# Score stack laid out heads, side, time: six two-sided transfers per batch instead of twelve

## The chip, the cores and the metric

The kernel runs on one core of a Trainium2 chip. The metric is device time in microseconds, the median of several runs. A profile of one more execution comes with it; its span goes from the first to the last instruction.

## The reference

Sixteen batches of a 128 x 256 array `x` pass through masked self-attention with 8 heads, then through a mixture of 8 experts of which the best one per token is taken, and the result is added to `x`. Only the attention's scores touch the change:

```python
q = xt @ Wq.T                                  # queries are keys and values too
scores = scale * einsum('bhqd,bhkd->bhqk', qh, qh)   # dk = 16
logits = (scores * cmask + (1.0 - cmask) * NEG) * rmask
attn = softmax(logits, axis=-1)
ctx  = einsum('bhqk,bhkd->bhqd', attn, qh)
out  = ctx @ Wo.T
...                                            # router, top expert, gate/up/down, x + result
```

## The kernel before

**Stages.** After a short opening comes the attention, a loop of 20 steps (`STEPS`) with eight head positions `h` in each, and after that the expert stage, 23 tiles of 128 tokens. Each engine has its own program written out by hand, and semaphores tie them; nothing is reordered by a scheduler. In step `s` TensorE (PE) computes the scores of batch `s` once to find the row maxima (`scores_for_max`, L572), the scores of batch `s - 2` a second time with mask and maximum folded in (`scores_for_exp`, L584), and the later products of batches `s - 2` to `s - 4`. VectorE (DVE) reduces the maxima (L930), ScalarE (ACT) takes the exponentials (L799) and GpSimd (POOL) splits the queries.

**The stack.** The scores are wanted in float32 precision from bfloat16 matmuls. The masked query `qm` of a batch is split into three bfloat16 parts (`parts`, by POOL at L310 to L316, for batch 0 by DVE at L916 to L922), and a tile `stack` holds in its first 96 partitions six slots of 16 rows. Slot `i` multiplies part `LEFT[i]` on the left side by part `RIGHT[i]` on the right side:

```python
LEFT = (0, 1, 2, 0, 0, 1)
RIGHT = (0, 1, 0, 1, 2, 0)
```

A row of the stack holds side, head, time. Each slot and side is one DMA within SBUF (`stack_part`, L437): SyncE's queue (SP) issues the six of the left side, ACT's queue the six of the right. There are five stacks (`NSTACK`). SP issues them in one row with everything else that it loads or stores: `x`, the mask for all partitions (`cond`), the stack's mask row (L468), the expert weights (L486 on), the hidden rows (L477) and, in steps 3, 7, 11 and 15, a copy of four batches of `x` from HBM to HBM (L481). ACT issues its own between exponentials.

**The maxima.** POOL splits a batch's maxima in two (`split_max`), PE turns them (L563, once in each step, at `h` = 2), DVE copies them to `max_rows` (L937), and ACT writes them with one DMA into rows 97 and 98 of the stack's right side (`write_max`, L827, at `h` = 3). `scores_for_exp` of that batch waits for them at `h` = 0 of the next step. In steps 0 and 1 PE runs fillers (`keep_warm`, L554) between the scores.

Of the kernel before, what the change touches and what calls it, by code (L numbers as in the profile page):

```python
# [7 lines left out]
F32 = mybir.dt.float32  # L8
BF16 = mybir.dt.bfloat16
# [3 lines left out]
ACT = mybir.ActivationFunctionType  # L13
AX = mybir.AxisListType

P = 128
NEG = -1e30
NH = 8
# [9 lines left out]
LEFT = (0, 1, 2, 0, 0, 1)  # L28
RIGHT = (0, 1, 0, 1, 2, 0)
ROWS = 6 * DK  # L30
ROW_MASK = ROWS
ROW_MAX = ROW_MASK + 1
ROWS2 = ROW_MAX + 2

NSTACK = 5
NPARTS = 4
NV = 3
NX = 4
# [4 lines left out]
def adaln_ffn(nc, x, cond, wqT, woT, routerT, guT, dnT, out):  # L43
    B, D, T = x.shape
# [4 lines left out]
    NT = T // P  # L49
# [21 lines left out]
    with ctx:  # L71
        def sb(name, shape, dt=F32):
            return ctx.enter_context(nc.sbuf_tensor(name, shape, dt))
# [7 lines left out]
        bank = [ctx.enter_context(nc.psum_tensor(f"bank{i}", [P, 512], F32)) for i in range(8)]  # L81
# [21 lines left out]
        dn2_sb = sb("dn2_sb", [P, E, T])  # L103

        cond_sb = sb("cond_sb", [B, T])
        mask2 = sb("mask2", [B, 2, NH, T], BF16)
        cond_all = sb("cond_all", [P, NCOND, T])
        x_sb = sb("x_sb", [P, NX, T])
        q_sb = sb("q_sb", [P, NQ, T])
        qm = sb("qm", [P, 2, T])  # L110
        rest = sb("rest", [P, 2, T])
        parts = sb("parts", [P, NPARTS, 3, T], BF16)
        stack = [sb(f"stack{r}", [P, 2, NH, T], BF16) for r in range(NSTACK)]
        v_sb = sb("v_sb", [P, NV, NT, NH, VC])
        row_max = sb("row_max", [P, 2, NH, NT])
        max_parts = sb("max_parts", [P, 2, P], BF16)
        max_rows = sb("max_rows", [2 * NH * NT, 2, P], BF16)
# [18 lines left out]
        start = sb("start", [P, E])  # L136
# [41 lines left out]
        rows_made = sem("rows_made")  # L178
# [10 lines left out]
        mask_made = sem("mask_made")  # L189
# [21 lines left out]
        max_in = sems("max_in", 2)  # L211
# [49 lines left out]
        def there(b):  # L261
            return 0 <= b < B
# [6 lines left out]

            return {0: 2, 1: 1}.get(b, b + 1)  # L270

        stack_rows = [stack[r][:, :, :, :].rearrange("p a h t -> p (a h t)").bitcast(F32) for r in range(NSTACK)]

        def home(n, first, end):

# [8 lines left out]
        def _(pool):  # L284
# [14 lines left out]
            def make_parts(b):  # L299
                k, r = b % 2, b % NPARTS  # L300
                pool.wait_ge(q_copied, q_count(b))
                pool.wait_ge(cond_all_in[b % NCOND], 16 * (b // NCOND + 1))
                if b == 2:
                    pool.wait_ge(first_parts, 2)
                g.tensor_tensor(qm[:, k, :], q_sb[:, b % NQ, :], cond_all[:, b % NCOND, :], ALU.mult).then_inc(qm_made, 1)  # L305
                pool.wait_ge(qm_made, b)
                if b >= NPARTS:
                    old = b - NPARTS
                    pool.wait_ge(stack_in[old % NSTACK], 16 * 12 * (old // NSTACK + 1))
                g.tensor_copy(parts[:, r, 0, :], qm[:, k, :]).then_inc(part0_made, 1)  # L310
                pool.wait_ge(part0_made, b)
                g.tensor_tensor(rest[:, k, :], qm[:, k, :], parts[:, r, 0, :], ALU.subtract).then_inc(rest_made, 1)
                g.tensor_tensor(parts[:, r, 1, :], qm[:, k, :], parts[:, r, 0, :], ALU.subtract).then_inc(parts_made, 1)
                pool.wait_ge(rest_made, b)
                pool.wait_ge(parts_made, 2 * b - 1)
                g.tensor_tensor(parts[:, r, 2, :], rest[:, k, :], parts[:, r, 1, :], ALU.subtract).then_inc(parts_made, 1)  # L316
# [114 lines left out]
                eng.wait_ge(qm_made, b - NCOND)  # L431
            eng.dma_start(cond_all[:, b % NCOND, :], cond[b:b + 1, :].to_broadcast([P, T])).then_inc(cond_all_in[b % NCOND], 16)

        def stack_part(eng, b, side, slot):

            part = (LEFT, RIGHT)[side][slot]
            eng.dma_start(stack[b % NSTACK][slot:ROWS:6, side, :, :],  # L437
                          parts[:, b % NPARTS, part, :]).then_inc(stack_in[b % NSTACK], 16)

        def need_parts(eng, b):  # L440
            if b == 0:
                eng.wait_ge(first_parts, 2)
            else:
                eng.wait_ge(parts_made, 2 * b)
            if b >= NSTACK:
                eng.wait_ge(s2_done, NH * (b - NSTACK + 1))

        def stack_first(eng, side):

            eng.wait_ge(first_hi, 1)  # L450
            for slot in range(6):
                if (LEFT, RIGHT)[side][slot] == 0:
                    stack_part(eng, 0, side, slot)
            for part in (1, 2):
                eng.wait_ge(first_parts, part)
                for slot in range(6):
                    if (LEFT, RIGHT)[side][slot] == part:
                        stack_part(eng, 0, side, slot)

        @block.sync  # L460
        def _(sp):
# [7 lines left out]

            def stack_parts(b):  # L470
                need_parts(sp, b)
                for slot in range(6):
                    stack_part(sp, b, 0, slot)

            def write_row(b):
                sp.wait_ge(gate_made, b + 1)
# [21 lines left out]
            stack_first(sp, 0)  # L498
            load_x(sp, 4)
            load_cond(sp, 4)  # L500
            need_parts(sp, 1)
            for slot in range(6):
                stack_part(sp, 1, 0, slot)
            stack_parts(2)
            for b in range(3):
                read_mask(b)
# [21 lines left out]
        def _(pe):  # L528
# [36 lines left out]
            def scores_for_max(b, h):  # L565
                k, n = b % NSTACK, NH * b + h
                if h == 0:
                    pe.wait_ge(stack_in[k], 16 * 12 * (b // NSTACK + 1))
                if n >= 2:
                    pe.wait_ge(max_done, n - 1)  # L570
                for q in range(NT):
                    mm = t_.matmul(bank[h % 2][:, q * T:(q + 1) * T], stack[k][0:ROWS, 0, h, q * P:(q + 1) * P],  # L572
                                   stack[k][0:ROWS, 1, h, :], start=True, stop=True)
                mm.then_inc(s1_done, 1)

            def scores_for_exp(b, h):
                k, n = b % NSTACK, NH * b + h
                if h == 0:
                    pe.wait_ge(max_in[b % 2], 16 * (b // 2 + 1))
                    pe.wait_ge(mask_in[k], 16 * (b // NSTACK + 1))  # L580
                if n >= 2:
                    pe.wait_ge(exp_done, n - 1)
                for q in range(NT):
                    mm = t_.matmul(bank[2 + h % 2][:, q * T:(q + 1) * T], stack[k][0:ROWS2, 0, h, q * P:(q + 1) * P],  # L584
                                   stack[k][0:ROWS2, 1, h, :], start=True, stop=True)
                mm.then_inc(s2_done, 1)

            def apply_probs(b, g):
# [184 lines left out]
        def _(act):  # L773
# [50 lines left out]
            def write_max(b):  # L824
                k = b % 2
                act.wait_ge(max_copied, b + 1)
                act.dma_start(stack[b % NSTACK][ROW_MAX:ROW_MAX + 2, 1, :, :], max_rows[:, k, :]).then_inc(max_in[k], 16)  # L827

            act.dma_start(wq_sb[:, :], wqT).then_inc(wq_in, 16)
            load_cond(act, 0)  # L830
# [7 lines left out]
            copy_q(2)  # L838
            act.wait_ge(cond_in, 16)
            all_heads = cond_sb[:, :].rearrange("b (o t) -> b o t", o=1).to_broadcast([B, NH, T])  # L840
            a.activation(mask2[:, 0, :, :], all_heads, ACT.Copy, bias=NEG, scale=-NEG).then_inc(mask_made, 1)
            a.copy(mask2[:, 1, :, :], all_heads).then_inc(mask_made, 1)
            need_parts(act, 1)
            for slot in range(6):
                stack_part(act, 1, 1, slot)

            for s in range(STEPS):
                for h in range(NH):
                    if there(s - 2):
                        exponential(s - 2, h)  # L850
                    if h < 2 and s >= 1 and there(s + 1):
                        stack_part(act, s + 1, 1, h + 4)
                    if h == 1 and there(s - 4):
                        copy_hidden(s - 4)
                    if h == 1 and there(s - 3):
                        copy_products(s - 3)
                    if h == 2 and there(s + 3):
                        copy_q(s + 3)
                    if h == 3 and there(s - 1):
                        write_max(s - 1)  # L860
                    if h >= 4 and there(s + 2):
                        if h == 4:
                            need_parts(act, s + 2)
                        stack_part(act, s + 2, 1, h - 4)
                    if h == 5 and there(s - 4):
                        exp_gap(s - 4)
                    if h == 5 and there(s):
                        copy_v(s)
                    if h == 6 and there(s - 3):
                        copy_context(s - 3)  # L870
# [33 lines left out]
        def _(dve):  # L904
# [1 line left out]
            minus_pair = float(np.frombuffer(np.array([0xBF80BF80], np.uint32).tobytes(), np.float32)[0])  # L906

            def minus_rows(k):
                v.memset(stack[k][ROW_MASK:P, 0, :, :].rearrange("p h t -> p (h t)").bitcast(F32), minus_pair).then_inc(rows_made, 1)

            minus_rows(0)
            dve.wait_ge(q_done, 1)
# [20 lines left out]
            def copy_max(b):  # L933
                dve.wait_ge(max_turned, b + 1)
                if b >= 2:
                    dve.wait_ge(max_in[b % 2], 16 * (b // 2))
# [301 lines left out]
```

## Time and profile before

| | us |
|---|---|
| median of 3 runs | 227.4 (227.11 to 230.67) |
| the profiled execution, its own time | 226.16 |
| its span | 224.3 |
| PE busy in the span | 208.8 (93%) |
| DVE, ACT, POOL busy | 145.8, 133.5, 113.9 |

The span is shorter than the execution's own time by 1.9 us that lie before its first and behind its last instruction. Busy times overlap. "SPq" and "ACTq" in the trace are the two engines' queues while they issue a DMA; an engine's queue issues in the program's order, and ACT's own instructions behind an issue start after it.

### The profile page before, as it was taken

Reading aid. Unit: us, or ns where it says so; the run is one execution under the profiler, and the core shown is the slowest. Engines: PE = TensorE matmul, PEld = TensorE weight load, DVE = VectorE, ACT = ScalarE, POOL = GpSimd, SP = SyncE. Lnnn points to the kernel's source line nnn. Section 1 sums busy time; section 2 is a strip of 40 time slices with the busy share of each in tenths; the row PEclk is TensorE's granted clock in tenths of the full one; section 3 lists DMA queues with packets and bytes.
Section 4 is the critical chain, followed back from the end, with each engine's and each line's share of the span. In section 5 each row is a group of like instructions: output and inputs, shape, how many; then the busy total and the mean of one; then the engine's idle time right before and its main releaser. Section 6 shows DMA issues by size and latency. Waiting matters only on the chain.

```text
span 224.3 us, 5401 instructions
## 1 busy us (share of the span) xinstructions
PE 208.8 (93%) x1723; PEld 149.5 (67%) x1723; DVE 145.8 (65%) x403; ACT 133.5 (60%) x298; POOL 113.9 (51%) x212
## 2 busy tenths in 40 slices
PE   6997989999999989999999999988899999999970
PEld 5996757767657747757766775446677777777750
DVE  2886977789789879889788884674763223322330
ACT  2260378888778868888887788772543343334310
POOL 5782775366266346346421001304617777777752
PEclk9999999999999999999999999999999999999995
DMA  6795575879699697786865450002716654543210
GB/s 167 183 187 139 122 211 140 229 214 255 160 226 236 174 254 197 183 222 168 242 195 125 134 157 24 27 27 58 238 43 182 195 147 143 157 138 96 93 43 0
DMA packets 44987, 34.39 MB, mean 153 GB/s; under 512 B 6220, under 2 KB 42975, under 8 KB 44960
## 3 DMA queue, kind: packets, MB, share of 16 engines
q1 hardware_dynamic: 26896, 18.77, 32.1%
q10 hardware_dynamic: 15120, 7.04, 12.9%
q0 software_dynamic: 2944, 8.24, 12.6%
q8 instruction: 15, 0.25, 0.5%
q14 instruction: 12, 0.10, 0.1%
HBM read 16.91 MB, written 7.28 MB: 108 GB/s over the span
## 4 chain that ended last, share of the span: by engine, by line
PE 74%; DMA 8%; DVE 5%; SPq 4%; issue 3%; ACT 2%; POOL 1%; ACTq 1%; POOLq 1%; DVEq 0%
PE bank L572 13%; PE bank L596 12%; PE bank L718 12%; PE bank L584 11%; PE bank L737 4%; PE bank L739 4%; PE bank L617 3%; SPq L437 3%; PE bank L539 2%; PE bank L625 2%; PE bank L606 2%; PE bank L729 2%; DMA stack<-max_rows 2%; DMA stack<-parts 2%; PE bank L709 2%
## 5 line engine op out<-in xcount | busy, mean ns | idle before, releaser
L930 DVE TENSOR_REDUCE row_max<-bank 128x2 f32<-128x512 f32 x128 | 85.2, 684 | 12.0 <-PE bank L572 10.6
L799 ACT ACTIVATE probs<-bank 128x512 f32<-128x512 f32 x128 | 75.5, 598 | 21.4 <-PE bank L584 18.1
L572 PE MATMUL bank<-stack 96*128 96x256 bf16 x256 | 49.4, 274 | 2.6 <-DMA stack<-parts 1.6
L584 PE MATMUL bank<-stack 99*128 99x256 bf16 x256 | 48.3, 272 | 0.9 <-DMA stack<-max_rows 0.8
L572 PEld LDWEIGHTS bank<-stack 96*128 96x128 bf16 x256 | 20.5, 97 | 22.3 <-DVE row_max L930 10.9
L596 PE MATMUL bank<-probs,v_sb 128*32 128x256 f32 x512 | 34.3, 385 | 0.2 <-ACT probs L799 0.2
L305 POOL TENSOR_TENSOR qm<-q_sb,cond_all 128x256 f32<-128x256 f32 x15 | 10.9, 729 | 39.6 <-ACT q_sb L784 38.0
L718 PE MATMUL bank<-gu_sb,gotT 128*128 x92 | 31.0, 460 | 0.0
L584 PEld LDWEIGHTS bank<-stack 99*128 99x128 bf16 x256 | 24.1, 97 | 7.1 <-ACT probs L799 2.9
L554 PE MATMUL bank<-ident 128*128 128x128 f32 x148 | 21.2, 286 | 1.8 <-POOL ident L289 1.6
L596 PEld LDWEIGHTS bank<-probs,v_sb 128*32 128x32 f32 x512 | 13.4, 109 | 12.7 <-ACT probs L799 4.7
L554 PEld LDWEIGHTS bank<-ident 128*128 128x128 f32 x148 | 19.2, 200 | 2.5 <-POOL ident L289 1.6
L718 PEld LDWEIGHTS bank<-gu_sb,gotT 128*128 128x128 f32 x92 | 15.8, 190 | 4.9
L882 ACT ACTIVATE silu<-bank 128x176 f32<-128x176 f32 x23 | 7.3, 317 | 19.5 <-PE bank L718 19.5
L1188 DVE SCALAR_TENSOR_TENSOR act_sb<-silu,stack,bank 128x176 f32<-128x176 f32 x15 | 6.0, 398 | 19.7 <-ACT silu L882 19.7
L401 POOL DMA_INDIRECT out<-stack,put_i x15 | 14.9, 994 | 6.3 <-issue 3.7
L876 ACT COPY gotT<-bank 128x256 f32<-128x256 f32 x23 | 8.6, 373 | 14.9 <-PE bank L709 14.9
L392 POOL DMA_INDIRECT stack<-rows_dram,take_i x15 | 14.5, 967 | 4.6 <-issue 3.7
L392 POOL DMA_INDIRECT got<-rows_dram,take_i x8 | 7.9, 982 | 17.3 <-DVE take_i L1085 9.8
L737 PE MATMUL bank<-dn_sb,actT 128*128 x46 | 13.7, 380 | 0.0
L739 PE MATMUL bank<-dn_sb,actT 128*128 x46 | 13.7, 379 | 0.0
L955 DVE MAX8 top<-h_sb 128x8 f32<-128x8 f32 x16 | 2.7, 170 | 15.2 <-ACT h_sb L818 15.2
(160 smaller groups left out, 316.5 us busy)
## 6 DMA issues: line engine op xcount, KB each, us to landing
stack<-parts SPq DMA_DIRECT2D x96, 64.0 KB, 3.0
stack<-parts ACTq DMA_DIRECT2D x96, 64.0 KB, 3.1
gu_sb<-in_guT SPq DMA_DIRECT2D x8, 352.0 KB, 3.9
rows_dram<-h_sb SPq DMA_DIRECT2D x16, 132.5 KB, 2.3
x_sb<-in_x SPq DMA_DIRECT2D x16, 128.0 KB, 3.7
rows_dram<-in_x SPq DMA_DIRECT2D x4, 512.0 KB, 5.2
cond_all<-in_cond SPq DMA_DIRECT2D x12, 128.0 KB, 4.7
dn_sb<-in_dnT SPq DMA_DIRECT2D x4, 256.0 KB, 3.9
```

What stands on the lines that cost most here:

```text
L305: g.tensor_tensor(qm[:, k, :], q_sb[:, b % NQ, :], cond_all[:, b % NCOND, :], ALU.mult).then_inc(qm_made, 1)
L392: g.indirect_dma_start(home(n, 0, ROW), None, rows, bass.IndirectOffsetOnAxis(ap=take_i[:, n:n + 1], axis=0)).then_inc(got_in[n], 16)
L401: g.indirect_dma_start(out_rows, bass.IndirectOffsetOnAxis(ap=put_i[:, n:n + 1], axis=0), home(n, XROW, ROW), None, bounds_check=TOK - 1, ...
L554: t_.matmul(bank[3][:, 0:P], ident[:, :], ident[:, :], start=True, stop=True)
L572: mm = t_.matmul(bank[h % 2][:, q * T:(q + 1) * T], stack[k][0:ROWS, 0, h, q * P:(q + 1) * P], stack[k][0:ROWS, 1, h, :], start=True, stop ...
L584: mm = t_.matmul(bank[2 + h % 2][:, q * T:(q + 1) * T], stack[k][0:ROWS2, 0, h, q * P:(q + 1) * P], stack[k][0:ROWS2, 1, h, :], start=True ...
L596: mm = t_.matmul(bank[PV][c * VC:(c + 1) * VC, g * T:(g + 1) * T], v_sb[:, b % NV, k, HG * g + c, :], probs[:, HG * g + c, k, :], start=(k ...
L718: mm = t_.matmul(bank[1 + m2][:, 0:I2], gotT[:, m2, k, :], gu_sb[:, k, bass.ds(e, 1), :].rearrange("p a i -> p (a i)"), start=(k == 0), st ...
L737: t_.matmul(bank[4 + m2][:, 0:T], actT[:, m2, 0, :], dn_sb[:, bass.ds(e, 1), :].rearrange("p a t -> p (a t)"), start=True, stop=False)
L739: t_.matmul(bank[4 + m2][:, 0:T], actT[:, m2, 1, :], dn2_sb[:, bass.ds(e, 1), :].rearrange("p a t -> p (a t)"), start=False, stop=True).th ...
L799: a.activation(probs[:, h, :, :].rearrange("p k t -> p (k t)"), bank[2 + h % 2][:, 0:NT * T], ACT.Exp, scale=float(DK) ** -0.5).then_inc(e ...
L930: v.tensor_reduce(row_max[:, b % 2, h, :], bank[h % 2][:, 0:NT * T].rearrange("p (q k) -> p q k", q=NT), AX.X, ALU.max).then_inc(max_done, 1)
```

## The change

A row of a stack now holds head, side, time. One DMA writes both sides of a slot, from the two parts that it names (`stack_slot`): six per batch, of which SP issues slots 0 to 2 and ACT slots 3 to 5. For batch 0 SP takes the even slots and ACT the odd ones. In ACT's loop the three stand at `h` = 5, 6 and 7 of step `s` for batch `s + 2`; before, four stood at `h` = 4 to 7 and two at `h` = 0 and 1 of the next step. The maxima of a batch now lie in two pieces of each head's row, and ACT writes them in two DMAs. Mask rows and fill follow the new order.

```diff
-        def stack_part(eng, b, side, slot):
-            part = (LEFT, RIGHT)[side][slot]
-            eng.dma_start(stack[b % NSTACK][slot:ROWS:6, side, :, :],
-                          parts[:, b % NPARTS, part, :]).then_inc(stack_in[b % NSTACK], 16)
+        def stack_slot(eng, b, slot):
+            left = parts[:, b % NPARTS, LEFT[slot], :]
+            both = bass.AP(left.tensor, left.offset, [left.ap[0], [(RIGHT[slot] - LEFT[slot]) * T, 2], left.ap[1]])
+            eng.dma_start(stack[b % NSTACK][slot:ROWS:6, :, :, :], both).then_inc(stack_in[b % NSTACK], 16)
...
-        def stack_first(eng, side):
-            eng.wait_ge(first_hi, 1)
-            for slot in range(6):
-                if (LEFT, RIGHT)[side][slot] == 0:
-                    stack_part(eng, 0, side, slot)
-            for part in (1, 2):
-                eng.wait_ge(first_parts, part)
-                for slot in range(6):
-                    if (LEFT, RIGHT)[side][slot] == part:
-                        stack_part(eng, 0, side, slot)
+        def stack_first(eng, part):
+            if part == 0:
+                eng.wait_ge(first_hi, 1)
+            for last in (1, 2):
+                for slot in range(part, 6, 2):
+                    if max(LEFT[slot], RIGHT[slot], 1) == last:
+                        eng.wait_ge(first_parts, last)
+                        stack_slot(eng, 0, slot)
...
-                act.dma_start(stack[b % NSTACK][ROW_MAX:ROW_MAX + 2, 1, :, :], max_rows[:, k, :]).then_inc(max_in[k], 16)
+                for q in range(NT):
+                    act.dma_start(stack[b % NSTACK][ROW_MAX:ROW_MAX + 2, :, 1, q * P:(q + 1) * P],
+                                  max_rows[q:2 * NH * NT:NT, k, :]).then_inc(max_in[k], 16)
...
-                    if h < 2 and s >= 1 and there(s + 1):
-                        stack_part(act, s + 1, 1, h + 4)
...
-                    if h >= 4 and there(s + 2):
-                        if h == 4:
+                    if h >= 5 and there(s + 2):
+                        if h == 5:
                             need_parts(act, s + 2)
-                        stack_part(act, s + 2, 1, h - 4)
+                        stack_slot(act, s + 2, SP_SLOTS + h - 5)
```

The two places that the prediction speaks of follow in the order of the instructions. The first is SP's opening, before: the loads of `x`, then the left sides of batch 0 (x6) and of batches 1 and 2 (x12), and those of batch 3 eight rows further down.

```order
L425 DMA x_sb<-in_x 128x256 x4
L437 DMA stack<-parts 16x8x256 x6
L425 DMA x_sb<-in_x 128x256
L432 DMA cond_all<-in_cond 128x256
L437 DMA stack<-parts 16x8x256 x12
L468 DMA stack<-mask 1x16x256 x3
L507 DMA wo_sb<-in_woT 128x128
...
L437 DMA stack<-parts 16x8x256 x6
L468 DMA stack<-mask 1x16x256
```

SP's opening now; the shape 16x16x256 is a slot with both sides.

```order
L426 DMA x_sb<-in_x 128x256 x4
L439 DMA stack<-parts 16x16x256 x3
L426 DMA x_sb<-in_x 128x256
L433 DMA cond_all<-in_cond 128x256
L439 DMA stack<-parts 16x16x256 x6
L467 DMA stack<-mask 1x16x256 x3
L504 DMA wo_sb<-in_woT 128x128
...
L439 DMA stack<-parts 16x16x256 x3
L467 DMA stack<-mask 1x16x256
```

The rows are the same and in the same order, with half as many stack transfers in each group.

The second place is ACT's row in one step of the loop, from the exponential at `h` = 3 to that at `h` = 7, before.

```order
L799 ACTIVATE probs<-bank 128x512
L827 DMA stack<-max_rows 2x16x128
L799 ACTIVATE probs<-bank 128x512
L437 DMA stack<-parts 16x8x256
L799 ACTIVATE probs<-bank 128x512
L437 DMA stack<-parts 16x8x256
L822 ACTIVATE gap_e<-gap 128x1
L792 COPY v_sb<-bank 128x16x16
L799 ACTIVATE probs<-bank 128x512
L437 DMA stack<-parts 16x8x256
L812 COPY cx_sb<-bank 128x264
L799 ACTIVATE probs<-bank 128x512
```

The same stretch now.

```order
L796 ACTIVATE probs<-bank 128x512
L825 DMA stack<-max_rows 2x8x128 x2
L796 ACTIVATE probs<-bank 128x512 x2
L439 DMA stack<-parts 16x8x512
L819 ACTIVATE gap_e<-gap 128x1
L789 COPY v_sb<-bank 128x16x16
L796 ACTIVATE probs<-bank 128x512
L439 DMA stack<-parts 16x16x256
L809 COPY cx_sb<-bank 128x264
L796 ACTIVATE probs<-bank 128x512
```

Two writes of the maxima follow each other ahead of the exponential at `h` = 4, and the stack transfer behind that exponential is gone. Slot 3 reads two neighbouring parts, so its pieces are 512 elements long (16x8x512).

## Rows read from the trace of the kernel before

**Rows 1.** The page: the span and part 1, busy time by engine.

```profile
span 224.3 us, 5401 instructions
PE 208.8 (93%) x1723; PEld 149.5 (67%) x1723; DVE 145.8 (65%) x403; ACT 133.5 (60%) x298; POOL 113.9 (51%) x212
```

**Rows 2.** Timeline of PE at h = 2: start, length, engine, line, tiles.

```profile
58.73 0.22 PE L563 MATMUL bank<-ident_b,max_parts 128*128 128x128 bf16 x1
...
67.48 0.22 PE L563 MATMUL bank<-ident_b,max_parts 128*128 128x128 bf16 x1
...
75.48 0.22 PE L563 MATMUL bank<-ident_b,max_parts 128*128 128x128 bf16 x1
...
84.41 0.22 PE L563 MATMUL bank<-ident_b,max_parts 128*128 128x128 bf16 x1
```

**Rows 3.** Timeline of PE, first scores of batches 0 and 1 (idle before, releaser).

```profile
11.60 0.38 PE L572 MATMUL bank<-stack 96*128 96x256 bf16 x2
...
19.31 0.39 PE L572 MATMUL bank<-stack 96*128 96x256 bf16 x2 [1.56 <-DMA stack<-parts]
```

**Rows 4.** The chain of waits in order of time, ahead of 19.31.

```profile
14.33 4.93 DMA stack<-parts
```

**Rows 5.** Timeline, weight load of batch 3's first scores.

```profile
32.43 0.11 PEld L572 LDWEIGHTS bank<-stack 96*128 96x128 bf16 x2 [0.92 <-DMA stack<-parts]
```

**Rows 6.** Timeline of ACT and its queue, around 57.

```profile
57.39 1.54 ACTq L437 DMA_DIRECT2D stack<-parts  x1
58.97 0.38 ACT L818 COPY h_sb<-bank 128x264 f32<-128x264 f32 x1 [0.99 <-issue]
```

**Rows 7.** The chain at 76.67, and the list of waits (total, times, longest).

```profile
76.67 5.03 DMA stack<-max_rows
...
PE bank L584 <- DMA stack<-max_rows: 0.8, 1, 0.8
```

**Rows 8.** Timeline of SP's queue, issues of stack parts, copy of x.

```profile
10.84 9.17 SPq L437 DMA_DIRECT2D stack<-parts  x12
...
26.02 4.19 SPq L437 DMA_DIRECT2D stack<-parts  x6
...
75.69 0.56 SPq L481 DMA_DIRECT2D rows_dram<-in_x  x1
```

**Rows 9.** Line L437, batch 0's issues (ns min/median/max), and landing.

```profile
L437 SPq DMA_DIRECT2D stack<-parts x6: 590/604/678, 5.8 to 9.1; - x6
...
DMA to landing us min/median/max: 2.0/2.1/2.6
```

**Rows 10.** Line L486, issues of 352 KB on SP (ns min/median/max).

```profile
L486 SPq DMA_DIRECT2D gu_sb<-in_guT x8: 434/510/702, 37.8 to 92.6; - x8
```

**Rows 11.** Timeline of DVE, parts 1 and 2 of batch 0.

```profile
6.14 0.95 DVE L919 TENSOR_TENSOR parts<-qm,parts 128x256 bf16<-128x256 f32 x1
7.20 0.43 DVE L922 TENSOR_TENSOR parts<-rest,parts 128x256 bf16<-128x256 f32 x1
```

**Rows 12.** Windows of 1 us; the last two columns are DMA share and GB/s.

```profile
8.00:9.00 1.00, 1.00 (x11) 1.00 (x10) 0.84 (x2) 0.00 (x0) 0.86 (x3) 1.00 0.82 210
...
14.00:15.00 1.00, 1.00 (x10) 0.92 (x9) 0.59 (x2) 0.40 (x2) 0.41 (x3) 1.00 1.06 266
```

**Rows 13.** Timeline of POOL, last part of batches 2 and 3.

```profile
13.22 0.67 POOL L316 TENSOR_TENSOR parts<-rest,parts 128x256 bf16<-128x256 f32 x1
...
17.40 0.67 POOL L316 TENSOR_TENSOR parts<-rest,parts 128x256 bf16<-128x256 f32 x1
```

**Rows 14.** Timeline of ACT and its queue, step 9, h = 3 and 4.

```profile
85.60 0.67 ACTq L827 DMA_DIRECT2D stack<-max_rows  x1
86.48 0.60 ACT L799 ACTIVATE probs<-bank 128x512 f32<-128x512 f32 x1 [0.28 <-PE bank L584]
```

**Rows 15.** Timeline of PE, second scores at h = 6 and at the next h = 0.

```profile
87.63 0.39 PE L584 MATMUL bank<-stack 99*128 99x256 bf16 x2
...
89.75 0.38 PE L584 MATMUL bank<-stack 99*128 99x256 bf16 x2
```

More of the change, by code:

```diff
@@ L35 @@
 NSTACK = 5
+SP_SLOTS = 3
 NPARTS = 4
@@ L105, in adaln_ffn @@
         cond_sb = sb("cond_sb", [B, T])
-        mask2 = sb("mask2", [B, 2, NH, T], BF16)
+        mask2 = sb("mask2", [B, NH, 2, T], BF16)
         cond_all = sb("cond_all", [P, NCOND, T])
@@ L112, in adaln_ffn @@
         parts = sb("parts", [P, NPARTS, 3, T], BF16)
-        stack = [sb(f"stack{r}", [P, 2, NH, T], BF16) for r in range(NSTACK)]
+        stack = [sb(f"stack{r}", [P, NH, 2, T], BF16) for r in range(NSTACK)]
         v_sb = sb("v_sb", [P, NV, NT, NH, VC])
@@ L270, in q_count @@
             return {0: 2, 1: 1}.get(b, b + 1)
-        stack_rows = [stack[r][:, :, :, :].rearrange("p a h t -> p (a h t)").bitcast(F32) for r in range(NSTACK)]
+        stack_rows = [stack[r][:, :, :, :].rearrange("p h a t -> p (h a t)").bitcast(F32) for r in range(NSTACK)]
         def home(n, first, end):
@@ L308, in make_parts @@
                     old = b - NPARTS
-                    pool.wait_ge(stack_in[old % NSTACK], 16 * 12 * (old // NSTACK + 1))
+                    pool.wait_ge(stack_in[old % NSTACK], 16 * 6 * (old // NSTACK + 1))
                 g.tensor_copy(parts[:, r, 0, :], qm[:, k, :]).then_inc(part0_made, 1)
@@ L471, in stack_parts @@
                 need_parts(sp, b)
-                for slot in range(6):
-                    stack_part(sp, b, 0, slot)
+                for slot in range(SP_SLOTS):
+                    stack_slot(sp, b, slot)
             def write_row(b):
@@ L500, in _ @@
             load_cond(sp, 4)
-            need_parts(sp, 1)
-            for slot in range(6):
-                stack_part(sp, 1, 0, slot)
+            stack_parts(1)
             stack_parts(2)
@@ L567, in scores_for_max @@
                 if h == 0:
-                    pe.wait_ge(stack_in[k], 16 * 12 * (b // NSTACK + 1))
+                    pe.wait_ge(stack_in[k], 16 * 6 * (b // NSTACK + 1))
                 if n >= 2:
@@ L571, in scores_for_max @@
                 for q in range(NT):
-                    mm = t_.matmul(bank[h % 2][:, q * T:(q + 1) * T], stack[k][0:ROWS, 0, h, q * P:(q + 1) * P],
-                                   stack[k][0:ROWS, 1, h, :], start=True, stop=True)
+                    mm = t_.matmul(bank[h % 2][:, q * T:(q + 1) * T], stack[k][0:ROWS, h, 0, q * P:(q + 1) * P],
+                                   stack[k][0:ROWS, h, 1, :], start=True, stop=True)
                 mm.then_inc(s1_done, 1)
@@ L578, in scores_for_exp @@
                 if h == 0:
-                    pe.wait_ge(max_in[b % 2], 16 * (b // 2 + 1))
+                    pe.wait_ge(max_in[b % 2], 32 * (b // 2 + 1))
                     pe.wait_ge(mask_in[k], 16 * (b // NSTACK + 1))
@@ L583, in scores_for_exp @@
                 for q in range(NT):
-                    mm = t_.matmul(bank[2 + h % 2][:, q * T:(q + 1) * T], stack[k][0:ROWS2, 0, h, q * P:(q + 1) * P],
-                                   stack[k][0:ROWS2, 1, h, :], start=True, stop=True)
+                    mm = t_.matmul(bank[2 + h % 2][:, q * T:(q + 1) * T], stack[k][0:ROWS2, h, 0, q * P:(q + 1) * P],
+                                   stack[k][0:ROWS2, h, 1, :], start=True, stop=True)
                 mm.then_inc(s2_done, 1)
@@ L840, in _ @@
             all_heads = cond_sb[:, :].rearrange("b (o t) -> b o t", o=1).to_broadcast([B, NH, T])
-            a.activation(mask2[:, 0, :, :], all_heads, ACT.Copy, bias=NEG, scale=-NEG).then_inc(mask_made, 1)
-            a.copy(mask2[:, 1, :, :], all_heads).then_inc(mask_made, 1)
+            a.activation(mask2[:, :, 0, :], all_heads, ACT.Copy, bias=NEG, scale=-NEG).then_inc(mask_made, 1)
+            a.copy(mask2[:, :, 1, :], all_heads).then_inc(mask_made, 1)
             need_parts(act, 1)
-            for slot in range(6):
-                stack_part(act, 1, 1, slot)
+            for slot in range(SP_SLOTS, 6):
+                stack_slot(act, 1, slot)
             for s in range(STEPS):
@@ L908, in minus_rows @@
             def minus_rows(k):
-                v.memset(stack[k][ROW_MASK:P, 0, :, :].rearrange("p h t -> p (h t)").bitcast(F32), minus_pair).then_inc(rows_made, 1)
+                v.memset(stack[k][ROW_MASK:P, :, 0, :].bitcast(F32), minus_pair).then_inc(rows_made, 1)
             minus_rows(0)
@@ L935, in copy_max @@
                 if b >= 2:
-                    dve.wait_ge(max_in[b % 2], 16 * (b // 2))
+                    dve.wait_ge(max_in[b % 2], 32 * (b // 2))
                 v.tensor_copy(max_rows[:, b % 2, :], bank[VM][:, :].bitcast(BF16)[0:2 * NH * NT, 0:P]).then_inc(max_copied, 1)
```

## The prediction

> **What bounds the kernel now.** I read the page first. PE is busy for 208.8 of 224.3 us [rows 1], so a gain must come out of the 15 us in which PE does nothing, and the question is how many of those the stack's transfers own. The chain of waits runs through PE nearly everywhere, so I went down PE's timeline for a mark that comes once per step, the turn of the maxima. From 67.48 to 75.48 is 8.00 us, the step of the undisturbed loop [rows 2]. No DMA ends a wait in such a step: its length is PE's own work with short waits for DVE and ACT, and fewer transfers cannot shorten it.
>
> Four places are longer, and a transfer or its issue ends each. (A) PE waits 1.56 us for batch 1's stack at 19.31 [rows 3]; the chain shows the last part issued at 14.33 and landed 4.93 us later [rows 4]. (B) The weight load of batch 3's first scores waits 0.92 us for its stack [rows 5]. (C) An issue on ACT's queue takes 1.54 us, ACT's next copy starts 0.99 us late [rows 6], and that step is 67.48 - 58.73 = 8.75 us, 0.75 over [rows 2]. (D) The maxima issued at 76.67 land after 5.03 us, the only one of sixteen that PE waits for [rows 7], and that step is 84.41 - 75.48 = 8.93 us, 0.93 over. Together they are 1.56 + 0.92 + 0.75 + 0.93 = 4.16 us. This is the ceiling of what the change can take out, 1.8% of the time.
>
> **What an issue costs.** An issue of 64 KB takes 0.60 us on a queue [rows 9], one of 352 KB takes 0.51 us [rows 10]. The cost goes by the instruction, not by the bytes, so I take 0.60 for the 128 KB of a whole slot. Per batch SP gives up three of six (1.8 us); ACT gives up three and takes one more for the maxima. The bytes stay: 6 x 128 KB = 786 kB per batch.
>
> **Opening, batch 0: a loss.** Before, the transfers began at 5.8 with the first part alone, and each landed within 2.0 to 2.6 us, so nothing queued behind anything [rows 9]. Now no slot starts before part 1 is made, 6.14 + 0.95 = 7.09 us [rows 11], and the slots with part 2 follow from 7.63 on. Both queues are through by about 7.1 + 3 x 0.64 = 9.05. The data then become the limit. The fastest rate near there is 266 GB/s with the engines full; with both queues issuing 64 KB pieces it is 210 GB/s at a share of 0.82 [rows 12]. So 786 kB take 2.95 to 3.7 us, and 1.75 us are fixed (the 2.0 of the quickest landing less 0.25 for its 64 KB). Batch 0 lands at 7.1 + 1.75 + 2.95 to 3.7 = 11.8 to 12.6 us, while PE starts it at 11.60 [rows 3] behind its fillers. That is a loss of 0.2 to 1.0; I take 0.6, the middle, since the two rates are equally near.
>
> **Opening, batch 1 (A).** Between batch 0 and batch 1 SP has two loads, 10.84 less the end of the sixth issue at 9.7, or 1.1 us [rows 8, 9]. It starts batch 1 at 10.2 and is done at 12.1, where before the sixth issue began at 14.33. Two batches and these two loads are 1835 kB; at the two rates they take 6.9 to 8.7 us, and the last lands at 15.8 to 17.6. PE asks for them at 19.31 - 1.56 = 17.75, plus the 0.6 of above, 18.35. The wait goes. What is late next is PE's own row of fillers and scores, so A is worth 1.56 - 0.6 = 1.0 us (0.5 to 1.4).
>
> **Opening, batch 3 (B).** Its last part is made at 18.07 [rows 13], yet SP issues it only from 26.02 to 30.21, behind twelve parts that held the queue until 20.01 [rows 8]. Now six slots stand there. Batch 2's part is made at 13.89 [rows 13], its three issues end by 15.9 instead of 20.01, and batch 3 follows at least 4 us earlier and ends sooner by another 2. Against a wait of 0.92 that is ample: B goes whole, 0.9.
>
> **The loop (C).** No row tells why that issue took 1.54 us. As the same bytes go through the same engines, it may come again, at another place, or not: 0 to 0.75, and I take 0.4.
>
> **The loop, the maxima (D and a new cost).** The second write is issued 0.67 + 0.04 = 0.71 us behind the first [rows 14], and PE needs both. In step 9 the first is issued at 85.60 and PE wants the rows at 89.75 [rows 14, 15], which leaves 4.15 us for one and 3.44 for the second. Fifteen of the sixteen landed without holding PE, hence within about 4.15; how far within, no row says. Per step the cost lies between nothing and 0.71. A little helps: ACT's last stack transfer now stands at `h` = 7, not at `h` = 1 just ahead of the maxima. Against it, SP is less full and will bring the copy of `x`, which in step 7 stood 1 us ahead of the slow write [rows 7, 8], close to the maxima in other steps too. I leave D as it is (0; -0.7 to 0.93 are its ends) and charge the other steps 0.3 together, near the lower end, since the mean landing of stack parts on an unqueued machine is 2.1 us [rows 9], well under 3.44.
>
> **The loop, ACT.** The exponential at `h` = 4 started at 86.48 [rows 14]. With two issues ahead of it, it starts at 85.60 + 2 x 0.71 = 87.02, ends at 87.62, and frees the bank that PE's second scores at `h` = 6 want at 87.63 [rows 15]. That is a tie, at worst 0.15 late with the semaphore and a weight load. Behind it the queue is lighter by one issue. Over 14 steps 0 to 2.1; I take 0.4.
>
> **The rest.** The strided fills, mask copies and matmul operands move as many elements in as many instructions, with 512-byte runs; I cost them nothing. They are covered by PE's fillers in the opening, and a slower fill would show as a later first reduction. The expert stage is not touched.
>
> **The sum.** 1.0 + 0.9 + 0.4 + 0 - 0.3 - 0.4 = 1.6 us out of the profiled execution's 226.16, so 224.6. That execution was 1.2 under the median of 227.4; against the median I predict 225.8 us.
>
> **Rivals.** (1) The transfers, not their issue, set the opening. The window from 14 to 15 us shows the engines full [rows 12], which speaks for it; batch 0's landings at 2.0 to 2.6 us without a queue [rows 9] speak against it. Then A and B stay, C too, and only the costs of 0.3 and 0.4 are left: 228.1. The Trainium skill (DMA: Bandwidth & Descriptors, section "Issuing engines are not separate DMA queues") says the same in general: all queues share the same 16 engines, and issuing from several saves only the sequencer's time, usually small beside the transfer. In the row an issue takes 0.60 us and 64 KB take 0.25 at the full rate, so here the issue is the larger; by the rule the sum would be nothing or a small loss. That a slot's issue takes twice as long, so that the change doesn't do what it says, ends at the same time; the 352 KB row speaks against that [rows 10].
> (2) Slower: the second write of the maxima holds PE in every step of the loop. It decides from a single landing of 3.44 us on; for it speaks the one of 5.03 [rows 7], against it that fifteen held nothing. At its worst it is 0.71 in 13 steps, 9.2 us; at half of that, 4.6, less the 2.3 gained, it ends at 229.7, and at the worst at 234.3.
> (3) All four places go, and batch 0 loses nothing: 227.4 - 4.2 = 223.2.
>
> **How the numbers follow.** My forecast (about 224.5 to 227) gets 0.55, rival 1 0.18, rival 2 0.12, rival 3 0.15. The range reaches to rival 3's 223.2, a little under it for the spread of the runs, and up past rival 1 to a half-sized rival 2: 222.8 to 229.4. Two per cent, about what a measurement of this kernel can tell from no change, is 4.5 us, more than the ceiling of 4.16. So faster by over 2% has 0.1, all from rival 3; slower by over 2% needs rival 2 near its worst, 0.06; the rest is 0.84.
>
> **What would show it.** Right: the wait before batch 1's first scores and that before batch 3's are gone; batch 0 starts between 11.8 and 12.6; an issue of a slot takes about 0.6 us; steps of the loop stay at 8.00. Wrong: issues of 1.2 us (rival 1's other form), a wait of PE on the maxima in most steps (rival 2), or a loop step shorter than 8.00, which would mean that ACT's or SP's issues had been in PE's way where I see none.

## The result and the profile after

The changed kernel is slower by 1.1%: 229.02 us (median of 8 runs, 228.16 to 231.07) against 227.25 us, a ratio of 1.0112 with an interval of 1.0075 to 1.0149. The forecast was 225.8, faster. Ratios here and below compare undisturbed runs only, so they need not be the quotient of two medians.

First the page of the changed kernel, the rows that answer to [rows 1], and its chain by line (the last line is cut at its end).

```profile
span 229.0 us, 5322 instructions
PE 211.2 (92%) x1723; PEld 148.9 (65%) x1723; DVE 145.9 (64%) x403; ACT 129.3 (56%) x298; POOL 114.1 (50%) x212
PE bank L593 12%; PE bank L569 12%; PE bank L715 12%; PE bank L581 11%; DMA stack<-max_rows 6%; PE bank L734 4%; PE bank L736 4%; PE bank L551 4%; PE bank L536 3%; PE bank L614 3%; PE bank L622 3%; PE bank L706 2%; PE bank L726 2%; PE bank 
```

The write of the maxima has 6% of the chain now (2% before). This profiled execution took 231.07 us, 4.9 more than the one of before; it is the slowest of the eight, so a second profile of the same kernel follows among the experiments.

PE's mark of each step, the turn of the maxima, answers to [rows 2].

```profile
34.59 0.22 PE L560 MATMUL bank<-ident_b,max_parts 128*128 128x128 bf16 x1
...
46.16 0.22 PE L560 MATMUL bank<-ident_b,max_parts 128*128 128x128 bf16 x1
...
54.16 0.22 PE L560 MATMUL bank<-ident_b,max_parts 128*128 128x128 bf16 x1
...
70.30 0.22 PE L560 MATMUL bank<-ident_b,max_parts 128*128 128x128 bf16 x1
...
79.95 0.22 PE L560 MATMUL bank<-ident_b,max_parts 128*128 128x128 bf16 x1
```

From 46.16 to 54.16 is the undisturbed 8.00 us, as before. From 34.59 to 46.16 is 11.57 (step 3) and from 70.30 to 79.95 is 9.65 (step 7); step 11 takes 9.00. PE's timeline says what it waited for in these three.

```profile
41.88 0.47 PE L581 MATMUL bank<-stack 99*128 99x256 bf16 x2 [1.79 <-DMA stack<-max_rows]
...
77.29 0.39 PE L581 MATMUL bank<-stack 99*128 99x256 bf16 x2 [1.48 <-DMA stack<-max_rows]
...
110.33 0.39 PE L581 MATMUL bank<-stack 99*128 99x256 bf16 x2 [0.84 <-DMA stack<-max_rows]
```

These are the steps with a copy of `x`. In the chain, the later write of the maxima lands 5.35 and 5.04 us after its issue in two of them, as the one slow write of before did [rows 7] (4.39 in step 11):

```profile
36.49 5.35 DMA stack<-max_rows
...
72.20 5.04 DMA stack<-max_rows
```

The queues around step 3 (start, length, queue, line) show what stood ahead.

```profile
34.51 0.62 SPq L467 DMA_DIRECT2D stack<-mask  x1
35.17 0.59 SPq L480 DMA_DIRECT2D rows_dram<-in_x  x1
35.78 1.40 ACTq L825 DMA_DIRECT2D stack<-max_rows  x2
35.80 0.62 SPq L485 DMA_DIRECT2D gu_sb<-in_guT  x1
```

SP issues the 512 KB copy at 35.17, and ACT issues the pair from 35.78 on. In step 7 the two stand at 71.15 and 71.49, in step 11 at 104.84 and 105.18. Before, SP ran up to a step behind ACT; one of the four copies fell within a microsecond ahead of a write, at 75.69 [rows 8]. With three issues fewer per batch SP keeps pace, and three of four do.

Step 3 lost more than its wait. The windows from the pair on (PE, PEld, DVE, ACT, POOL, then the granted clock, DMA share, GB/s) show full DMA engines from 38 us on, and behind the wait the clock.

```profile
36.00:38.00 2.00, 2.00 (x19) 1.62 (x17) 1.97 (x5) 1.09 (x3) 1.86 (x4) 1.00 0.73 211
38.00:40.00 2.00, 2.00 (x24) 0.96 (x24) 1.03 (x3) 1.60 (x5) 1.73 (x3) 1.00 1.11 264
40.00:42.00 2.00, 0.21 (x3) 0.11 (x2) 0.98 (x2) 0.50 (x1) 0.41 (x2) 1.00 1.01 257
42.00:43.00 1.00, 1.00 (x4) 0.64 (x3) 0.00 (x0) 0.60 (x1) 0.00 (x0) 0.53 1.19 221
43.00:44.00 1.00, 1.00 (x5) 0.46 (x3) 0.30 (x1) 0.00 (x0) 0.00 (x0) 0.50 1.13 211
44.00:45.00 1.00, 1.00 (x13) 0.52 (x16) 0.39 (x1) 0.87 (x2) 0.00 (x0) 0.50 1.05 173
```

PE was busy for 0.21 of 2 us, and then TensorE was granted 0.50 of its full clock, 1.2 instead of 2.4 GHz, for some three microseconds. Its work took longer there: the two matmuls of L622 at 42.14 took 1.09 us, in step 4 they took 0.61. That is where 3.57 us over the 8.00 come from, with a wait of 1.79.

The opening, against [rows 3 and 5]:

```profile
12.83 0.39 PE L569 MATMUL bank<-stack 96*128 96x256 bf16 x2 [1.27 <-DMA stack<-parts]
...
18.83 0.38 PE L569 MATMUL bank<-stack 96*128 96x256 bf16 x2
...
30.08 0.39 PE L581 MATMUL bank<-stack 99*128 99x256 bf16 x2 [0.58 <-ACT probs L796]
```

In this pair of profiles batch 0 starts 1.23 us later than before, batch 1 starts 0.48 earlier and without a wait, and nothing waits for batch 3's stack. The opening varies between executions, so these two sizes are taken up again below with the profiles of the experiments. A new wait of 0.58 us stands in step 2, for an exponential. Line L439 shows the issue of a whole slot (ns min/median/max), against [rows 9]:

```profile
L439 ACTq DMA_DIRECT2D stack<-parts x48: 558/616/1684, 6.9 to 125.9; - x48
L439 SPq DMA_DIRECT2D stack<-parts x48: 570/630/1801, 7.0 to 119.9; - x48
```

### The profile page after: what moved, and what is told of

Same layout as the page of the kernel before. It is cut to its first block, busy times and chain, and to the rows that moved or that the text cites. A ratio compares the mean times of both kernels' runs of the same rounds, so it can differ in the third digit from the quotient of the medians.

```text
span 229.0 us, 5322 instructions
## 1 busy us (share of the span) xinstructions
PE 211.2 (92%) x1723; PEld 148.9 (65%) x1723; DVE 145.9 (64%) x403; ACT 129.3 (56%) x298; POOL 114.1 (50%) x212
## 4 chain that ended last, share of the span: by engine, by line
PE 77%; DMA 10%; DVE 3%; ACT 2%; issue 2%; POOL 1%; POOLq 1%; SPq 1%; ACTq 0%
PE bank L593 12%; PE bank L569 12%; PE bank L715 12%; PE bank L581 11%; DMA stack<-max_rows 6%; PE bank L734 4%; PE bank L736 4%; PE bank L551 4%; PE bank L536 3%; PE bank L614 3%; PE bank L622 3%; PE bank L706 2%; PE bank L726 2%; PE bank L603 2%; ACT probs L796 2%
## 5 line engine op out<-in xcount | busy, mean ns | idle before, releaser
L796 ACT ACTIVATE probs<-bank 128x512 f32<-128x512 f32 x128 | 73.9, 599 | 31.0 <-PE bank L581 29.0
L581 PE MATMUL bank<-stack 99*128 99x256 bf16 x256 | 48.8, 275 | 4.8 <-DMA stack<-max_rows 4.1
L593 PE MATMUL bank<-probs,v_sb 128*32 128x256 f32 x512 | 35.0, 392 | 0.2 <-ACT probs L796 0.2
L581 PEld LDWEIGHTS bank<-stack 99*128 99x128 bf16 x256 | 22.5, 98 | 15.2 <-ACT probs L796 6.6
L803 ACT COPY pv_sb<-bank 128x512 f32<-128x512 f32 x16 | 9.4, 585 | 4.3 <-PE bank L593 4.3
```

The source lines that it names most:

```text
L593: mm = t_.matmul(bank[PV][c * VC:(c + 1) * VC, g * T:(g + 1) * T], v_sb[:, b % NV, k, HG * g + c, :], probs[:, HG * g + c, k, :], start=(k ...
L796: a.activation(probs[:, h, :, :].rearrange("p k t -> p (k t)"), bank[2 + h % 2][:, 0:NT * T], ACT.Exp, scale=float(DK) ** -0.5).then_inc(e ...
```

## The experiments

Two theories. **C**: the writes of the maxima wait on the DMA engines behind what SP issued just ahead of them, the copy of `x` above all; the change moved that traffic there. **W**: the second write is too late by itself, whatever SP issues. "Steps of the loop" are steps 3 to 12, from one turn of the maxima to the next. The eleven kernels ran on three chips, in groups of four, four and three; each has its own runs of the kernel before beside it.

| kernel | median us | before, same chip | ratio (95%) |
|---|---|---|---|
| e1_copies_late | 226.10 | 226.99 | 1.0007 (0.9960 to 1.0053) |
| e2_one_write | 230.27 | 226.99 | 1.0170 (1.0084 to 1.0257) |
| e3_before_two_writes | 231.15 | 226.99 | 1.0233 (1.0157 to 1.0308) |
| e4_before_copies_late | 226.25 | 226.99 | 1.0028 (0.9984 to 1.0071) |
| e5_before_two_late | 227.71 | 225.61 | 1.0082 (1.0045 to 1.0120) |
| e6_loads_behind_max | 225.88 | 225.61 | 0.9994 (0.9960 to 1.0028) |
| e7_copy_behind_max | 226.73 | 225.61 | 1.0043 (1.0012 to 1.0074) |
| e8_behind_max_late | 224.63 | 225.61 | 0.9951 (0.9919 to 0.9982) |
| e9_before_behind_late | 225.81 | 225.74 | 0.9982 (0.9948 to 1.0016) |
| e10_after_again | 228.47 | 225.74 | 1.0125 (1.0086 to 1.0165) |
| e11_slot0_first | 224.21 | 225.74 | 0.9935 (0.9907 to 0.9964) |

**e10_after_again: the same kernel, a second profile.**

> The changed kernel once more, unaltered, for a second profile and for times beside the others on one chip. Theory C: again the long steps are those in which SP's traffic (a copy of x or loads) was issued within about 1.5 us ahead of the maxima; a ratio of 1.005 to 1.015. If the long steps of the first profile were chance, they are gone and the ratio is 1.00.

The loss is there again, 1.0125. Steps 3, 7 and 11 are again the long ones, 9.14, 9.10 and 8.71 us, and all the others of the loop are 7.99 or 8.00. The clock stayed at full in them. The list of waits (the fourth is one of 0.23 us in step 2), and step 3's queue and wait:

```profile
PE bank L581 <- DMA stack<-max_rows: 2.7, 4, 1.0
...
35.85 0.59 SPq L480 DMA_DIRECT2D rows_dram<-in_x  x1
36.22 1.39 ACTq L825 DMA_DIRECT2D stack<-max_rows  x2
...
41.50 0.39 PE L581 MATMUL bank<-stack 99*128 99x256 bf16 x2 [0.98 <-DMA stack<-max_rows]
```

The copies stand 0.37, 0.20 and 0.32 us ahead of the pair. So it is no chance of one execution.

**e1_copies_late: the changed kernel without the copies in these steps.**

```diff
-                if s % 4 == 3 and there(s - 3):
-                    write_x(s - 3)
+                if 14 <= s < 18:
+                    write_x(4 * (s - 14))
```

> The changed kernel with the four copies of x (HBM to HBM, 512 KB each) issued in steps 14 to 17 instead of 3, 7, 11 and 15; nothing else differs. Theory C (the copy): SP, relieved of three issues per batch, now issues the copy just ahead of the write of the maxima, which queues behind it on the DMA engines, and PE waits. Then no write of the maxima holds PE by over 0.3 us in steps 3, 7 and 11, these steps are 8.0 to 8.2 us (11.58, 9.65 and 9.00 now), and the time is 224 to 226. Theory W (the second write): the pair itself is too late, whatever is copied. Then PE still waits 0.5 us and more for the maxima in several steps and the time stays at 228 to 229.

The ratio falls to 1.0007, so the copies made some 1.1% of loss by where they stood. Steps 7 and 11 are 7.99 and 8.00. But step 3 is still 9.07 with a wait of 0.90, and step 8 is 8.75. The time, no better than before, is 226.10, just above C's range and far from W's. C as I put it, with the copy alone, falls short. In both steps no copy stands near; other loads do. In step 3 a load of 352 KB was issued at 35.11, 0.34 us ahead of the pair. The rows of step 8 (the second write is the x2 row's):

```profile
75.79 0.58 SPq L476 DMA_DIRECT2D rows_dram<-h_sb  x1
...
76.42 0.43 SPq L485 DMA_DIRECT2D gu_sb<-in_guT  x1
76.76 1.39 ACTq L825 DMA_DIRECT2D stack<-max_rows  x2
76.90 0.51 SPq L426 DMA_DIRECT2D x_sb<-in_x  x1
...
81.66 0.39 PE L581 MATMUL bank<-stack 99*128 99x256 bf16 x2 [0.59 <-DMA stack<-max_rows]
```

A load of 352 KB ahead is not enough by itself: in step 5 one stands 0.33 us ahead of the pair too, and no matmul waits (one weight load does, for 0.27 us). The engines' share in the three microseconds from 35, 76 and 52 us on was 0.99 to 1.22 (step 3), 0.55 to 0.82 (step 8) and 0.56 to 0.85 (step 5), so it does not tell step 8 from step 5. What decides between these two stays open.

**e6_loads_behind_max: SP's loads behind the maxima in each step.**

```diff
                     read_mask(s + 2)
+                if there(s - 1):
+                    sp.wait_ge(max_in[(s - 1) % 2], 32 * ((s - 1) // 2 + 1))
                 if there(s - 5):
```

> The changed kernel, with SP waiting in each step for the landing of the maxima before it issues the hidden rows, the copy of x, the expert weights and the next x and mask. Both writes, the layout and the copies' steps stay. Theory C: nothing of SP's stands ahead of the maxima any more, PE waits for them nowhere by over 0.2 us, all steps of the loop are 8.0 to 8.2, and the time is 223.5 to 225.5. Theory W: the second write, 0.71 later, still holds PE in several steps: 227 to 229.

0.9994: the 1.2% are back, with both writes in place, though 225.88 us is above the 225.5 of C's range. Steps 3, 7 and 11 are 7.99 to 8.00. Two waits of PE are over C's 0.2: one of 0.86 us in step 1, before the loop, and one of 0.53 us in step 8, at 80.96, which made that step 8.70. The copy of step 7 was issued at 71.28, behind the maxima, with a load of 352 KB, `x` and mask after it; the engines were still full from 75 to 79 us, when step 8's pair was issued (76.12). That the copy made this wait is a reading of the order; in e8, where no copy stands there, it is gone.

**e7_copy_behind_max: only the copy, in its four steps.** The same wait stands directly ahead of `write_x`, under its condition.

> The changed kernel, with SP waiting for the landing of the maxima only ahead of the copy of x, in steps 3, 7, 11 and 15. Theory C: the waits in steps 3, 7 and 11 fall from 1.79, 1.48 and 0.84 us to under 0.3, and the time is 224 to 226. Theory W: they fall by the copy's share only and 0.7 remains in each; 226.5 to 228.

1.0043, and 226.73 us lies in W's range, not in C's. The waits tell another story: those in steps 3, 7 and 11 went, as C has it and W does not, but others came in the steps after: step 4 is 9.21 us and step 8 is 8.62. The copies were issued some 2.5 us behind their pair, at 38.22 and 71.51; as I read it, their traffic then met the next one.

```profile
49.05 0.39 PE L582 MATMUL bank<-stack 99*128 99x256 bf16 x2 [1.04 <-DMA stack<-max_rows]
```

**e8_behind_max_late: both cures.** The edits of e1_copies_late and e6_loads_behind_max together.

> The changed kernel with SP's loads behind the maxima in each step and the copies of x in steps 14 to 17, the two cures together. Theory C: as with the loads alone, 223.5 to 225.5, at most 0.5 us less, since a copy behind the maxima holds nobody. Theory W: 227 to 229.

0.9951, faster than before. Every step from 3 to 12 is 7.98 to 8.00 us, and no matmul of PE waits for the maxima, though both writes are in place. So W falls for the new layout: with SP's loads and copies out of the way, the pair is in time. SP's stack slots and mask still stand ahead of it. SP's queue shows the pause between mask and hidden row. In the windows (last two columns DMA share and GB/s) the engines are full in the first microsecond of the pair, issued at 77.10, and nearly empty in the next two.

```profile
75.74 0.62 SPq L467 DMA_DIRECT2D stack<-mask  x1
79.61 0.33 SPq L476 DMA_DIRECT2D rows_dram<-h_sb  x1
...
77.00:78.00 1.00, 1.00 (x12) 0.94 (x10) 0.96 (x3) 0.62 (x2) 0.83 (x2) 1.00 1.12 184
78.00:79.00 1.00, 1.00 (x11) 0.92 (x9) 1.00 (x4) 0.41 (x1) 0.92 (x2) 1.00 0.22 37
79.00:80.00 1.00, 1.00 (x13) 0.42 (x15) 0.97 (x5) 0.98 (x4) 0.86 (x3) 1.00 0.06 12
```

**e2_one_write: one write again, in the new layout.** PE turns the two halves apart, so that the rows need no splitting. POOL's split and DVE's copy follow the new order; the cut leaves them out.

```diff
-                t_.transpose(to[:, 0:P], max_parts[:, b % 2, :], ident_b[:, :]).then_inc(max_turned, 1)
+                for q in range(NT):
+                    mm = t_.transpose(to[0:P // NT, q * P:(q + 1) * P], max_parts[:, b % 2, q * P // NT:(q + 1) * P // NT],
+                                      ident_b[:, :])
+                mm.then_inc(max_turned, 1)
...
+                act.dma_start(stack[b % NSTACK][ROW_MAX:ROW_MAX + 2, :, 1, :], max_rows[:, k, :]).then_inc(max_in[k], 16)
```

> The changed kernel with the maxima of a batch in one write of 2 x 8 x 256 (PE turns the two halves apart, two turns of 64 columns in place of one of 128); copies of x as they are. Theory C: a single write behind the copy lands 4.2 to 5.0 us after its issue, as the first of the pair does now (4.97, 5.05 and 4.2), so PE still waits 0.4 to 0.9 us in steps 3 and 7; the time is 226 to 228. Theory W: the waits go, all steps are 8.0 to 8.2, and the time is about 225.

230.27, outside both theories, because the edit has a cost of its own: the undisturbed step is 8.31 us instead of 8.00, in all of the loop. DVE's copy of the rows got longer, 269 ns where it was 202, and PE, which is busy for all of that step, has a second turn:

```profile
L936 DVE COPY max_rows<-bank 16x256 bf16<-16x256 bf16 x8 | 2.2, 269 | 0.0
...
84.97 0.38 PE L585 MATMUL bank<-stack 99*128 99x256 bf16 x2
85.29 0.30 PE L562 MATMUL bank<-ident_b,max_parts 128*64 128x128 bf16 x2
85.52 0.70 PE L537 MATMUL bank<-x_sb,wq_sb 128*128 128x256 f32 x2
86.05 0.38 PE L573 MATMUL bank<-stack 96*128 96x256 bf16 x2
...
93.60 0.30 PE L562 MATMUL bank<-ident_b,max_parts 128*64 128x128 bf16 x2
```

The growth of 0.31 lies at PE's turn: from the score ahead of it to the first score behind it PE takes 1.08 us here (84.97 to 86.05) and 0.76 in e10 (85.03 to 85.79). Why two turns cost that much more is not settled. Against its own 8.31, step 3 is still 0.86 over, with a wait for the single write of 0.83 us. The copy was issued at 35.52, 0.05 us behind that write (35.47), so it need not stand ahead to hold a write up; the size is C's number. But steps 7 and 11, with the copy 0.64 and 0.76 us ahead, are only 0.01 and 0.33 over, and step 5, without a copy, is 0.51 over; the three steps with copies lose 1.2 us together, where two writes lost 2.95 in the second profile. So the second write has its part in the loss too. How much of it, this run can't say, as its steps are longer.

**e3_before_two_writes: two writes in the old layout.** The loop over two halves of `write_max`, with `1, :, q * P:(q + 1) * P` as the target.

> The kernel before with only the maxima written in two transfers (halves of each head's row), all else as before. Theory C: only where a copy stands ahead of the write, step 7, the wait grows by up to 0.7 us; the other steps stay at 8.00, and the time is 227.0 to 228.2. Theory W: PE waits for the maxima in several more steps and the time is at least that of the changed kernel, 229 or more.

231.15, a ratio of 1.0233, so as W forecast and far from C's 227 to 228.2. In the profile the place is C's, one step and not several:

```profile
43.49 0.60 SPq L481 DMA_DIRECT2D rows_dram<-in_x  x1
44.13 0.62 SPq L486 DMA_DIRECT2D gu_sb<-in_guT  x1
...
45.11 1.38 ACTq L828 DMA_DIRECT2D stack<-max_rows  x2
...
51.52 0.55 PE L584 MATMUL bank<-stack 99*128 99x256 bf16 x2 [2.10 <-DMA stack<-max_rows]
```

A copy and a load stand ahead of the pair, PE waits 2.10 us, and the clock falls behind that too. This one step, step 4, takes 11.89 us, 3.89 over the 8.00; it is the only wait of PE for the maxima in that profile.

**e4_before_copies_late: one write, no copies, old layout.** The edit of e1_copies_late in the kernel before.

> The kernel before with the four copies of x issued in steps 14 to 17. Theory C: the one step in which PE waited for the maxima, 75.48 to 84.41, falls from 8.93 to 8.0, and the time is 226.0 to 226.6. Theory W: with one write there is nothing to wait for but chance; the step stays where it is or the wait moves, and the time is 227 to 227.5.

The step with place D falls to 8.00, as C has it, and every step from 4 to 10 is 7.99 to 8.08. The time is 226.25 against 226.99, the ratio 1.0028 and its interval spans 1, so no gain can be claimed. Its profile has another loss, a wait of 1.76 us for batch 3's stack at 33.94: place B again, in the old order of SP's opening.

**e5_before_two_late: two writes, no copies, old layout.** Both edits.

> The kernel before with the maxima in two writes and the copies of x in steps 14 to 17, to be held against the same kernel with one write and late copies (226.25). Theory C (a write of the maxima waits behind what SP has put on the DMA engines just ahead of it): without the copies the second write costs 0 to 1 us, 226.2 to 227.3, with a wait of PE here and there behind other loads. Theory W (the second write is too late by itself): it keeps its 4 us, 230 to 231.

1.0082 (227.71), between the two theories, and in its profile PE waits for the maxima nowhere. The longest step of the loop has another cause, place C:

```profile
58.24 1.57 ACTq L437 DMA_DIRECT2D stack<-parts  x1
59.85 0.38 ACT L818 COPY h_sb<-bank 128x264 f32<-128x264 f32 x1 [1.03 <-issue]
```

An issue of ACT's at `h` = 1 takes 1.57 us and the copy of the hidden rows starts late; that step is 8.93 us. The four kernels of the old layout, each against the kernel before on its chip, are: one write with copies 1, one write without them 1.0028, two writes with copies 1.0233, two without 1.0082. So two writes cost 2.3% where the copies stand and less, about half a per cent by runs on two chips, where they don't, and the copies cost nothing that shows beside one write. The loss there takes both. What the half per cent is, with no wait for the maxima in the profile, stays open.

**e9_before_behind_late: the cures without the change.** e8's two edits in the kernel before (waits of 16 for the single write).

> The kernel before with the same two cures: SP's loads behind the landing of the maxima in each step, copies of x in steps 14 to 17. If the change gives SP the room that this wait needs, the kernel before has none: its SP issues stack parts until late in the step, the loads slip, and the stack lands late; 227 to 229, slower than before. If the cures alone make the gain and the change adds nothing, it is as fast as the changed kernel with both cures, a ratio of 0.995 to before.

0.9982, its interval spans 1: not slower, as I had thought, so the kernel before has room for this wait as well. The other forecast, 0.995, lies within its interval, so this run alone does not tell the cures from the change; the next one, on the same chip, goes further. Its long steps are 9.11 and 8.53; ahead of the first an issue on ACT's queue at 57.69 takes 1.90 us, place C once more.

**e11_slot0_first: the best version.** e8, and slot 0 of batch 0 no longer waits for part 1.

```diff
-                        eng.wait_ge(first_parts, last)
+                        if max(LEFT[slot], RIGHT[slot]) > 0:
+                            eng.wait_ge(first_parts, last)
                         stack_slot(eng, 0, slot)
```

> The changed kernel with both cures, and slot 0 of batch 0, which needs part 0 alone, issued as soon as that part is made, some 1.3 us before part 1. If the first scores wait for the amount of data behind 7.1 us, batch 0 starts 0.3 to 0.6 us earlier and the time is 0.3 to 0.6 us under that of the two cures; if they wait for the slots with part 2, nothing changes.

0.9935 (224.21), the fastest of all, 0.7% under the kernel before and 1.9% under the changed kernel on the same chip. It is also 1.6 us under e9, which has the cures without the change (225.81). Its loop is 7.98 to 8.00 throughout, with one wait of PE for the maxima, 0.48 us in step 2. Batch 0 starts at 11.84 with its first transfer issued at 5.85; in the other profiles of the new layout it starts between 12.44 and 14.21. On e8 it gains 0.16 points, within the intervals; e8 ran on another chip.

## Why the prediction was wrong

**The step that failed is "The loop, the maxima".** I left place D as it was and charged 0.3 us to all other steps. The three steps with copies lose 3.57 + 1.65 + 1.00 = 6.2 us in the first profile and 1.14 + 1.10 + 0.71 = 2.95 in the second, where before had D's 0.93. Over D's 0.93 and the 0.3 charged, that alone takes more than the 1.6 us of gain. I had named both parts: the margin that falls from 4.15 to 3.44 us, and an SP that brings the copy close to the maxima in other steps too. The price was wrong since I took the landing of an unqueued stack part, 2.1 us [rows 9], for writes that queue. The row to take was the 5.03 behind a copy [rows 7]: 5.03 + 0.71 - 4.15 = 1.6 us, in each step in which SP keeps pace, that is in steps 3, 7 and 11 as now, 4.8 us in all, between the two profiles. I also called D's place step 7. The copy is SP's of step 7, but ACT and PE stood in step 8 by then: that SP lagged by a step could be read there, and with it what would follow if it stopped. C holds with "copy" widened to SP's loads (e1, e6, e8); W, by which the pair is late by itself, fell with e8. The second write is no bystander, though: in the old layout the loss takes both it and the copies. Rival 2 was the right side with the wrong place: not every step, but some of those in which SP's traffic stands ahead.

**Opening, batch 0 and A.** The direction was right: batch 0 starts later, batch 1 earlier, and its wait is gone. The first pair of profiles has a loss of 1.23 for batch 0 (0.6 taken, at most 1.0) and a net 0.48 for A where I had 1.0. But the opening varies by more than that. Over all profiles without e11 (the edits of the others lie behind this point), batch 0 starts at 12.44 to 14.21 now (seven, median 12.69; the sign I had named was 11.8 to 12.6) and at 11.60 to 14.15 before (five, median 12.13), a loss of 0.56; the turn of batch 0's maxima, two microseconds behind batch 1's first score, comes at a median of 20.68 now and 21.69 before, a gain of 1.0. By the medians both terms were near what I took, and the 0.48 is one draw. A wait for batch 1's stack stands in four of the five profiles of the old layout (1.04 to 1.60 us) and in none of the eight of the new one. The six slots of batch 0 landed 2.7 to 4.1 us after their issue, so they queued on the engines as said.

**Opening, B.** The wait for batch 3 is gone, as forecast; in the old layout it stands in two of five profiles (before and e4), so 0.9 was too much for a mean. Part of what it gave was eaten by a term that I had in another place.

**The loop, ACT.** I took 0.4 over 14 steps. The loop's steps stay at 8.00, so it costs nothing there; step 2, which is shorter, has it in full, the 0.58 us wait for the exponential behind two issues. With it the turn of step 3 comes at 34.59 and in the second profile at 35.02, against 34.87 before, so the opening as a whole gained about nothing in these two. In the other profiles the same turn comes at 33.94 to 35.94 now and at 35.17 to 37.44 before.

**The loop, C.** I gave it half. It goes nearly in full: no stack issue stands ahead of the hidden copy at `h` = 1 any more. In each of the five profiles of the old layout ACT starts a copy 0.5 to 1.4 us late behind an issue, at `h` = 1 or elsewhere; in the new one only e2 has such a place behind the opening (0.93 us).

**What an issue costs** was right: 0.62 us for 128 KB. With that the second form of rival 1 falls, an issue twice as long; its first form, in which A and B stay, falls with their waits, which are gone. Its 228.1 is near the result by chance. With the cures on both sides, e11 against e9 on one chip, the change is worth 1.6 us, part of it from slot 0. That is the 1.6 that I had summed up, but from terms of which ACT's and B's were off, so the agreement is in part luck.

## What to carry to other kernels

A queue that is freed does not idle: it issues what comes next in its row, earlier. Before taking work off it, look at which small, late-bound transfer of another queue its next large one will now precede, and price that by the slowest landing that the trace shows behind such a load. A wait that orders the large one behind the small one cost nothing that shows here, neither in the new layout (e6, e8) nor in the old one (e9).

## What was unexpected of the hardware

A write of the maxima, 8 KB in one or 4 KB each in two, took 4.1 to 5.7 us to land where another queue had issued 512 KB 0.2 to 1.6 us ahead of the first of them, in the nine cases that the chain shows (it shows only writes that held PE), so a separate queue did not carry it past them. And a wait of PE cost more than its length: behind 1.79 us in the changed kernel, 2.10 in e3 and 1.76 in e4, the clock was granted at about half for 3.4 us, while it stayed at full behind the 1.48 us of step 7.
